# Two GNN layers on one core: in the first histogram, the one-hot rows of one tile in four are built on POOL by comparisons, not on ACT by distances

## What is computed

```
x = layernorm(x + GAT(x, edge_index=[src, dst], edge_attr_32))     # attention over incoming edges, 4 heads
x = layernorm(x + GNN(x, edge_attr_128, senders=src, receivers=dst))  # MLP per edge, gated, mean over senders

# GAT:  x_proj = x @ lin_W.T;  att = s_src[src] + s_dst[dst] + edge term;  softmax over the edges of each dst
#       out = segment_sum(x_proj[src] * alpha, dst)
# GNN:  h = tanh(tanh([x[src], x[dst]] @ W0 + b0) @ W1 + b1) @ W2 + b2;  h *= edge_attr_128 @ Wg
#       out = segment_sum(h, src) / max(count(src), 1)
```

## Time and profile before

| | |
|---|---|
| median of 3 runs | 5223.99 us (5223.35 to 5227.84) |
| the profiled execution's own time | 5231.43 us |
| its span | 5229.3 us, the clock granted 0.927 on average |
| busy shares over the whole span | PE 79%, DVE 73%, ACT 63%, POOL 62% |

### The profile page before, as it was taken

The page is one execution under the profiler, slowest core; times in us unless marked ns, Lnnn a source line. Parts: engine busy times, 40 slices in busy tenths (PEclk is TensorE's granted clock), DMA queues, the critical chain, the costliest instruction groups (busy, mean ns, idle before and its releaser), DMA issues. The chain is left out here.

```text
span 5229.3 us, 101877 instructions
## 1 busy us (share of the span) xinstructions
PE 4150.3 (79%) x24476; PEld 3393.8 (65%) x24476; DVE 3817.4 (73%) x12104; ACT 3302.5 (63%) x7255; POOL 3246.6 (62%) x3026
## 2 busy tenths in 40 slices
PE   5688888888577774999999979999999999999300
PEld 3455555555344444999999968787878778778200
DVE  5787787788577776989899847666666666666564
ACT  6866666666344442666666647777767777767475
POOL 0067667677666664555555537777777777877332
PEclk9999999999788886999999989999999999999655
DMA  3233333333476656999999966666666666666596
GB/s 78 38 99 100 92 99 100 94 98 99 111 186 177 180 176 202 371 354 367 358 361 366 352 215 149 147 149 153 150 149 149 153 148 151 148 148 153 147 393 273
DMA packets 774602, 971.45 MB, mean 186 GB/s; under 512 B 181969, under 2 KB 685816, under 8 KB 761656
## 3 DMA queue, kind: packets, MB, share of 16 engines
q0 software_dynamic: 169856, 322.79, 27.8%
q10 hardware_dynamic: 268637, 374.18, 19.8%
q1 hardware_dynamic: 336055, 273.89, 17.0%
HBM read 541.99 MB, written 429.17 MB: 186 GB/s over the span
## 5 line engine op out<-in xcount | busy, mean ns | idle before, releaser
L1359 PE MATMUL bank<-w0r,n_x1T 128*128 128x406 f32 x4704 | 904.7, 351 | 37.5 <-ACT n_pa L1407 35.3
L1359 PEld LDWEIGHTS bank<-w0r,n_x1T 128*128 128x128 f32 x4704 | 869.6, 190 | 60.9 <-ACT n_pa L1407 58.5
L1506 POOL DMA_INDIRECT out_x<-u_sums,u_row x392 | 649.4, 1657 | 143.0 <-issue 107.6
L1558 PE MATMUL bank<-u_h,w1r 128*108 128x512 f32 (+1 forms) x2646 | 706.2, 413 | 0.0
L593 POOL DMA_INDIRECT DS<-by_dst,rank_int x392 | 376.1, 959 | 425.0 <-DVE rank_int L747 320.1
L1235 POOL DMA_INDIRECT n_cg<-CT,n_last x392 | 446.7, 1140 | 176.7 <-issue 95.3
L1558 PEld LDWEIGHTS bank<-u_h,w1r 128*108 128x108 f32 (+1 forms) x2646 | 453.4, 178 | 134.1
L817 POOL DMA_INDIRECT xg<-XP,m_src x392 | 398.0, 1015 | 193.3 <-issue 95.7
L1488 POOL DMA_INDIRECT u_pa<-PA,u_rows x392 | 383.6, 979 | 170.3 <-issue 116.2
L1558 PE MATMUL bank<-w2r,u_h 108*128 108x256 f32 x3528 | 478.8, 280 | 0.0
L599 POOL DMA_INDIRECT DS<-r_s_dst,r_head_rows x392 | 388.2, 990 | 119.5 <-issue 119.5
(11 more groups left out here) (282 smaller groups left out, 10501.5 us busy)
## 6 DMA issues: line engine op xcount, KB each, us to landing
PA<-n_pa ACTq DMA_DIRECT2D x98, 816.0 KB
PB<-n_pb ACTq DMA_DIRECT2D x98, 812.0 KB
XP<-xps ACTq DMA_DIRECT2D x98, 528.0 KB
CT<-ct ACTq DMA_DIRECT2D x98, 528.0 KB
n_xp<-XP SPq DMA_DIRECT2D x98, 528.0 KB
xin<-in_x SPq DMA_DIRECT2D x97, 512.0 KB, 4.6
n_x<-in_x SPq DMA_DIRECT2D x97, 512.0 KB, 9.5
out_x<-n_x ACTq DMA_DIRECT2D x97, 512.0 KB, 4.6
```

The source lines that it names most:

```text
L1359: o = nc.tensor.matmul(acc, xT[s][p][:, k, e], w0r[q][:, 2 * half + k, :], start=(n == 0), stop=(n == len(terms) - 1))
L1506: pool.indirect_dma_start(out=out, out_offset=bass.IndirectOffsetOnAxis(ap=si[s][:, j:j + 1], axis=0), in_=yo[s][:, j, :], in_offset=None, ...
L1558: o = nc.tensor.matmul(acc, a[p], b[q], start=(start and n == 0), stop=(stop and n == 2))
```

## The change

POOL gets a `body` of its own in this block, and ACT loses `one_hot`. For each group POOL waits for `h_acc` = g - 1, copies the two digits of tile 3 into a small buffer `key_pair` (`pk`, 128 x 2), waits for these copies, and then does for tile 3 what DVE does for the others: a comparison over 128 columns and one over 392, with the digit as a scalar for each partition. It counts in `h_ohp`, which PE waits for where it waited for `h_oha`.

```
@@ -404,7 +405,7 @@
-                h_oha = sem("h_onehot_act")
+                h_ohp = sem("h_onehot_pool")
@@ -438,6 +439,22 @@
                         nc.gpsimd.memset(far[:], -BIG).then_inc(h_pad, 1)
+                        pool.wait_ge(h_chain, KEYS_READY)
+
+                        def body(g, s, i, last):
+                            c = Count(pool, h_ohp)
+                            c.at(3 * g)
+                            need(pool, h_acc, g - 1)
+                            pool.sem_inc(turn, 1)
+                            for k, digit in enumerate((LO, HI)):
+                                c.did(nc.gpsimd.tensor_copy(pk[s][:, k:k + 1], digit[0][:, bass.ds(g * G + G - 1, 1)]))
+                            c.wait()
+                            pool.sem_inc(turn, 1)
+                            for k, w in enumerate((slice(0, P), slice(P, OW))):
+                                o = nc.gpsimd.tensor_scalar(oh[0][s][:, G - 1, w], iota[:, 0:w.stop - w.start],
+                                                            pk[s][:, k:k + 1], None, ALU.is_equal)
+                            c.did(o)
+                        groups(pool, body)
@@ -456,7 +473,7 @@
-                            pe.wait_ge(h_oha, 3 * (g + 1))
+                            pe.wait_ge(h_ohp, 3 * (g + 1))
@@ -533,24 +550,11 @@
-                        def one_hot(g, s):
-                            c = Count(act, h_oha)
-                            c.at(3 * g)
-                            need(act, h_acc, g - 1)
-                            distances(c, g, G - 1, 0, away[s][:, 0, :])
-                            c.wait()
-                            c.did(nc.scalar.activation(oh[0][s][:, G - 1, :], away[s][:, 0, :], ACT.Relu,
-                                                       bias=ones[:, 0:1], scale=-1.0))
-
                         def body(g, s, i, last):
-                            if not late(g, 1):
-                                one_hot(g + 1, 1 - s)
                             keep_e(g)
                             if not late(g, 1):
                                 copy_e(g + 1, 1 - s)
                         copy_e(0, 0)
-                        act.wait_ge(h_chain, KEYS_READY)
-                        one_hot(0, 0)
                         groups(act, body)
```

More of the change, by code:

```diff
@@ L397, in gnn_kernel @@
                 hist = alloc(ph, "hist", [P, NT])
+                pk = [alloc(ph, f"key_pair{s}", [P, 2]) for s in range(2)]
                 tot = [alloc(ph, f"tot{q}", [P, NT]) for q in range(2)]
```

## The result

The changed kernel takes 5281.82 us (median of 4 runs, 5279.68 to 5285.86); the kernel before took 5223.67 beside it. The ratio is 1.0112, with an interval of 1.0095 to 1.013: 58 us slower, 50 to 68 by the interval. The forecast was 5249, 25 us slower: right in its direction, less than half of the size.

What follows compares the result with a forecast made beforehand. ACT was taken to bound the histogram at 1.79 us a group; POOL and DVE sharing SBUF would make it 2.05, 0.26 more over 97 groups: 5224 + 25 = 5249 us, with an 8-in-10 range of 5182 to 5300.

Steps and rivals of the forecast that it cites:

- What bounds the kernel now: Histogram loop: ACT sets the period of 1.79 us a group; PE and DVE follow it.
- The part that is removed: ACT's three one-hot instructions for tile 3 go, 1.58 us of its 1.79; the period could fall to 1.30 at best.
- The part that is added: POOL's copies, wait and two comparisons, priced at 0.29 and 0.50 us, make a chain of 1.32 us a group.
- Rival 4: POOL's comparison costs double a cast's price per column: 2.46 us a group, 65 us slower, 5289 us; chance 0.10.
- What it does to DVE: POOL's two comparisons exclude DVE's (0.79 us), its copies by 0.07: 1.19 + 0.79 + 0.07 = 2.05 us a group.
- The sum: Histogram period 2.05 - 1.79 = 0.26 us a group more, over 97 groups 25 us slower.
- rival 1: POOL and DVE hardly meet; POOL's undisturbed 1.32 us sets the period: 46 us faster, 5178 us; chance 0.27.
- The start: Before the first products: POOL's first tile ready at about 46.3 against 46.82 with ACT, no loss worth a term.
- The end: After the last products the block goes on as before and later blocks are untouched.
- rival 2: POOL is late, not DVE, whose delays hide in slack: 1.88 us a group, 9 us slower, 5233 us; chance 0.19.
- Rival 3: POOL's and DVE's instructions exclude each other end to end: 2.42 us a group, 61 us slower, 5285 us; chance 0.11.
- What would show it: Trace signs: ACT about 20% busy, period 2.05, DVE's six comparisons stretched some 0.8 us, POOL's at 0.3 and 0.5 us.

Runs made afterwards that it cites:

- the last version: Kernel before with tile 3's low-digit row on DVE and high-digit row on ACT, timed again: 5868.1 us against 5896.05, ratio 0.9941.
- The price list: Kernel before plus POOL instruction forms timed alone, then the change's POOL copies and comparisons, unused, in every second group: 5218.53 us beside 5226.75, single run.
- the kernel that alternates: Kernel before with tile 3 of even groups from POOL and of odd groups from ACT: 5246.86 us, ratio 1.0047.

## Why the prediction came out at half the loss

- **What bounds the kernel now**: right. ACT set the period; taking a part of its work away (the last version) brought 31 us in the block.
- **The part that is removed**: right. ACT's share fell to 18% of the stretch (about 20% was forecast), and no engine waits long for `eT` any more.
- **The part that is added: this step failed.** "I take 0.29 and 0.50 for the comparisons, since the select costs what the cast does." They measured 0.64 and 1.26, and from the start of the first to the next group's copy 1.83 us, where 0.76 stood in the chain. Per column it is 2.4 ns and not 0.78. The select is another form of instruction, and its row bore witness only for itself. The upper end that was kept, a doubled price, was still below the true one; and the end above it, the power's row at 145 ns a column, was left out. The price list shows that the form of the instruction is what costs. Rival 4 held this doubt, with a chance of 0.10, and it didn't move the forecast.
- **What it does to DVE**: half right. DVE's comparisons of 392 columns have a mean of 0.417 instead of 0.31, and a longest of 0.647; the meeting does occur in every group. The durations of the six grow by 3 x (0.255 + 0.417) - 1.69 = 0.33 us together, where some 0.8 were forecast. It was charged to the period besides, where it doesn't appear: DVE has 0.76 us of waiting a group, and the price-list kernel kept its period of 1.793 under the same stretching.
- **The sum** therefore had the wrong form too. It added DVE's work and POOL's. With the true prices it gives 1.19 + 1.90 + 0.07 = 3.16 us; measured 2.34. What holds is POOL's own chain, copies and their wait 0.50 and comparisons 1.83, that is 2.33. Two errors of opposite sign left 25 of the 58 us. That even the direction came out was luck: with POOL's own chain as the period and the assumed prices, 1.32 us, the forecast would have been rival 1's 46 us faster.
- **The start** was "no loss worth a term"; it lost 2.3 us, again by the price of the first comparisons, 2.87 us for the two. **The end** was to go on as before; it lost some 2.7 us, of which 2 go to the lower clock.
- **The rivals**: the mechanism is that of rival 2 (POOL is the late one, DVE's delays hide in its slack) at the price of rival 4 (and above it, triple and not double). Rival 3's 5285 lies nearest to the measured time, but its mechanism isn't there: DVE's comparisons run at 0.31 to 0.34 in the middle of POOL's, and the engines' work doesn't add up. By the rule of the Trainium skill (SBUF — State Buffer, "Who interferes with whom"), taken as the prediction took it, that DVE's comparisons use both ports, they would have been blocked for the whole instruction; the rows below disagree. Which mode they run in no run here shows.
- **What would show it**: the text said that POOL's comparisons at 0.4 and 0.9 us would speak for rival 4. They were beyond.

## What to carry to other kernels

Price a new instruction by its own form on its own engine; where the trace has none, give a dearer price a real chance and let it move the forecast, because another form with the same shape may be two and a half times cheaper (a cast of 392 columns 0.50 us, the comparison 1.26). When two engines work in parallel and meet in memory, ask first which of them is waited for: the other's delays cost only beyond its slack, and only the critical engine's longer instructions reach the time. Before work goes to an idle but slow engine, look whether the excess fits into the waiting time of a fast one.

## What the runs showed of the hardware

- **POOL's tensor-scalar form** costs 2.4 ns a column and 0.3 us fixed: 0.61 us for 128 columns, 1.26 for 392, for a comparison as for a subtraction, at 16 and 32 bits, 1.19 with a constant. A copy of 392 takes 0.52 to 0.57. These lengths are real and not only printed: the comparison added to the changed kernel takes 0.60 and lengthens the period by 0.62. The Trainium skill (GPSIMD Engine Reference, "Engine selection") calls streaming work with one input roughly line-rate on this engine; the copy bears that out better than the comparison.
- **DVE is held by POOL in two stretches of an instruction, not all through it.** Timeline of the kernel with one more comparison on POOL:

```profile
149.90 1.26 POOL L456 TENSOR_SCALAR onehot<-iota,key_pair 128x392 f16<-128x392 f16 x1
149.91 0.62 DVE L344 TENSOR_SCALAR onehot<-iota,key_lo 128x128 f16<-128x128 f16 x1 [1.18 <-PE bank L481]
150.45 0.31 DVE L345 TENSOR_SCALAR onehot<-iota,key_hi 128x392 f16<-128x392 f16 x1
150.68 0.53 DVE L344 TENSOR_SCALAR onehot<-iota,key_lo 128x128 f16<-128x128 f16 x1
```

  POOL works from 149.90 to 151.16. The DVE instruction that starts with it takes 0.62 instead of 0.25; the next, from 0.55 to 0.86 into it, its usual 0.31; the third, at 0.78, lasts until POOL is done. From 60 to 200 us the trace has 47 such groups, all with these three durations to 0.01 us. What the two stretches are (reading and writing, perhaps) was not tested.
- **Products at half the rate under a printed clock of 1.00: the record is missing, not the rate wrong.** Four products take 0.83 us in the earlier trace rows and 1.49 here: their starts are (0.83 - 0.33) / 3 = 0.17 us apart against (1.49 - 0.53) / 3 = 0.32. 392 columns in these times are the upper level of the clock, 2.4 GHz, and the lower, 1.2. A single product lasts 329 ns by the median before and 531 to 534 in the kernels whose period POOL or the slowed ACT sets. But the printed granted clock of the stretch is 0.57 in the changed kernel, and 1.00 in the one with a slow ACT, shown above, and in the one with more on POOL, whose products last as long. The trace's own records of the clock say why. They don't begin with the span: the first, at the upper level, stands at 60.7 us in the kernel before, at 60.1 in the changed one, at 282.5 with the slow ACT and at 339.9 with more on POOL, behind the last product there. The column takes off what the records show as lost, so it prints 1.00 where there is none. In all thirteen traces no product as short as 0.33 us stands more than 0.1 us ahead of the first record; the products at 46.82 in the earlier trace rows and at 49.09 above are examples, four in 1.47 us under a printed 1.00. So in these stretches the clock was at its lower level and the 1.00 is a missing record; a matmul's own duration tells its rate. In this change the lower level costs nothing in the loop, because PE waits for POOL either way, and 2 us at the end of the block; in the kernel that alternates it lengthens a round trip in which PE does count.
